# Attention and feed-forward layer on eight cores: order of score tiles in attention, queue of the reciprocal rows' write, PSUM banks of the down projection

## What is computed

```python
x = x + layernorm(attn(layernorm(x), w_qkv, w_out))
x = x + layernorm(ffn(layernorm(x), gate, up, down))
# attn: qkv = x @ w_qkv.T; per head and chunk of 512 queries, keys are the
# chunk before and its own (1024 keys; chunk 0 has 512); band mask
# j >= i and j <= i + 512; softmax(q k^T / sqrt(128)) @ v; then @ w_out.T
# ffn: W = (wq - 128) * scale; down(silu(gate(x)) * up(x))
```

## Time and profile before

| | us |
|---|---|
| runs shown | 4037.57 and 4462.24, median 4249.91 |
| the profiled execution | 4037.43 |
| its span, slowest core (core 1) | 4035.9 |
| spans of the eight cores | 4006.8 to 4035.9 |
| TensorE busy in the span | 3283.2 (81%) |
| VectorE, ScalarE, POOL busy | 1188.4, 813.9, 154.4 |

### The profile page before, as it was taken

How to read it: one execution, slowest core, us unless ns; L and a number is a source line. 1 busy time by engine, 2 the same in 40 slices (tenths; PEclk the granted TensorE clock), 3 DMA queues, 4 the chain that set the end, 5 groups by cost and what they waited for, 6 DMA issues and landing times.

```text
span 4035.9 us, 41674 instructions; the slowest of 8 cores (4006.8 to 4035.9 us)
## 1 busy us (share of the span) xinstructions
PE 3283.2 (81%) x16208; PEld 1526.1 (38%) x16208; DVE 1188.4 (29%) x1421; ACT 813.9 (20%) x1175; POOL 154.4 (4%) x208
## 2 busy tenths in 40 slices
PE   2578898898888843666599999999999869949886
PEld 1334444444444421233244444444444324414332
DVE  3434423423433443565511111111101111122223
ACT  1223323323323320212211111111111210020000
POOL 0000000000000000000000000000000000000000
PEclk9789999999999976887799999999999979979998
DMA  5221121121030034433211111111111233225655
GB/s 168 84 64 31 50 67 28 50 68 28 10 110 6 29 102 146 144 138 132 104 42 37 42 42 37 42 39 40 32 27 39 58 107 116 98 73 199 222 213 185
DMA packets 174800, 328.00 MB, mean 81 GB/s; under 512 B 9104, under 2 KB 131344, under 8 KB 154128
## 3 DMA queue, kind: packets, MB, share of 16 engines
q1 hardware_dynamic: 138128, 162.26, 13.1%
q0 software_dynamic: 23232, 115.36, 8.7%
q10 hardware_dynamic: 13248, 47.72, 3.5%
HBM read 243.38 MB, written 81.92 MB: 81 GB/s over the span
## 4 chain that ended last, share of the span: by engine, by line
PE 68%; DMA 13%; DVE 9%; issue 7%; ACT 2%; DVEq 0%; ACTq 0%; SPq 0%; POOL 0%; POOLq 0%
PE ps L871 15%; PE ps L889 15%; PE ps L388 11%; PE ps L950 9%; PE ps L347 6%; DMA ys<-SM 4%; PE ps L604 3%; DVE SM L593 3%; PE ps L518 2%; PE ps L528 2%; PE ps L697 2%; DMA CF<-ys 2%; PE ps L580 2%; DMA recs<-RCS 2%; DMA CF<-wdT 2%
## 5 line engine op out<-in xcount | busy, mean ns | idle before, releaser
L871 PE MATMUL ps<-AT,BB 128*128 128x512 bf16 x2816 | 617.8, 380 | 5.6 <-DVE BB L847 5.6
L889 PE MATMUL ps<-AT,BB 128*128 128x512 bf16 x2816 | 615.0, 379 | 0.0
L950 PE MATMUL ps<-BB,AT 128*128 128x512 bf16 x2048 | 466.8, 390 | 158.0 <-DVE SM L824 106.7
L388 PE MATMUL ps<-AT,BB 128*128 128x512 bf16 x2048 | 469.2, 383 | 2.5 <-ACT BB L398 2.5
L543 DVE TENSOR_REDUCE STT<-ps 128x1 f32<-128x1024 f32 (+1 forms) x256 | 268.0, 1087 | 630.0 <-PE ps L528 630.0
L871 PEld LDWEIGHTS ps<-AT,BB 128*128 128x128 bf16 x2816 | 276.4, 98 | 339.8 <-issue 9.6
L889 PEld LDWEIGHTS ps<-AT,BB 128*128 128x128 bf16 x2816 | 275.4, 98 | 332.4
L950 PEld LDWEIGHTS ps<-BB,AT 128*128 128x128 bf16 x2048 | 204.0, 100 | 417.8 <-issue 191.0
L697 PE MATMUL ps<-BB,SM 128*128 128x512 bf16 x1024 | 255.7, 416 | 114.0 <-ACT SM L716 99.6
L904 DVE TENSOR_TENSOR SM<-SM 128x2048 bf16<-128x2048 bf16 x44 | 53.9, 1225 | 980.6 <-ACT SM L899 980.6
L550 ACT ACTIVATE SM<-ps,STT 128x1024 bf16<-128x1024 f32 (+1 forms) x256 | 258.0, 1008 | 253.3 <-DVE STT L543 238.6
(11 more groups left out here) (92 smaller groups left out, 1872.3 us busy)
## 6 DMA issues: line engine op xcount, KB each, us to landing
AT<-zTs SPq DMA_DIRECT2D x32, 1408.0 KB, 9.0
CF<-wqkvT SPq DMA_DIRECT2D x36, 1024.0 KB, 10.5
CF<-x POOLq DMA_DIRECT2D x32, 1024.0 KB, 7.0
zTs<-SM POOLq DMA_DIRECT2D x44, 512.0 KB, 4.8
CF<-woutT SPq DMA_DIRECT2D x16, 1024.0 KB, 6.2
CF<-recs ACTq DMA_DIRECT2D x16, 1024.0 KB, 4.8
x1s<-SM POOLq DMA_DIRECT2D x16, 1024.0 KB, 5.0
ys<-SM POOLq DMA_DIRECT2D x32, 512.0 KB, 4.9
```

The lines of the kernel that those rows point to most:

```text
L388: ins = e.matmul(ps1[:, _nn * 512:(_nn + 1) * 512], _w[:, k * P:(k + 1) * P], h1T(k, _h2 * 1024 + _nn * 512, 512), start=(k == 0), stop=(k ...
L871: ins = e.matmul(ps0[:, n * 512:(n + 1) * 512], BB[:, (_base + k // 4) * 2048 + (k % 4) * 512 + _htl * P: (_base + k // 4) * 2048 + (k % 4 ...
L889: ins = e.matmul(ps1[:, n * 512:(n + 1) * 512], BB[:, (_base + k // 4) * 2048 + (k % 4) * 512 + _htl * P: (_base + k // 4) * 2048 + (k % 4 ...
L950: ins = e.matmul(_pso[:, n * 512:(n + 1) * 512], _zz[:, kt * P:(kt + 1) * P], wd_ap(kt)[:, n * 512:(n + 1) * 512], start=(kt == 0), stop=( ...
```

## The change

Three edits. In attention, the loop over tiles is cut into `emit_smm` (scores) and `emit_soft` (maximum and exponential). A chunk now emits: scores of tiles 0 and 1; the transposes and V product of the chunk before; a fill unit; softmax of tiles 0 and 1; a fill unit; scores of tiles 2 and 3; softmax of tiles 2 and 3. Banks, tiles and instructions stay as they are. In the projection, the write of the reciprocal row is issued by POOL instead of SP. In the down projection, row tiles alternate between banks 0, 1 and banks 2, 3 instead of going through all four pairs.

```diff
-                for t in range(4):
+                def emit_smm(t):
...
                     tr.emit("PE", smm,
                             reads=[qT_pg, kT_pg, rMK, rIDB], writes=sc_bks)
 
+                def emit_soft(t):
+                    reg = (t % 2) * 1024
+                    sc_bks = [bank[2 * (t % 2)], bank[2 * (t % 2) + 1]]
...
-                    if t == 1:
-                        drain_fill(1)
-
+
+                emit_smm(0)
+                emit_smm(1)
                 flush_tp()
                 drain_fill(1)
+
+                emit_soft(0)
+                emit_soft(1)
+                drain_fill(1)
+                emit_smm(2)
+                emit_smm(3)
+                emit_soft(2)
+                emit_soft(3)
...
-            dma("SY", rec_d[st2].rearrange("(a c) -> a c", a=16),
+            dma("GP", rec_d[st2].rearrange("(a c) -> a c", a=16),
                 RCS[0:16, :], "recw", reads=[rRCS],
...
-                q4 = st % 4
-                pb = [bank[2 * q4], bank[2 * q4 + 1]]
-                pso = (ps0 if q4 < 2 else ps1)[
-                    :, (q4 % 2) * 1024:(q4 % 2) * 1024 + 1024]
+                pb = bank[0:2] if st % 2 == 0 else bank[2:4]
+                pso = ps0[:, 0:1024] if st % 2 == 0 else ps0[:, 1024:2048]
```

## The result

The kernel became slower: the ratio of its time to that of the kernel before is 1.0384, with a 95% interval of 1.0366 to 1.0402. The median of the eleven executions is 4191.39 us; the profiled one took 4184.07 us around a span of 4182.5 us, 146.6 us more than the profiled execution before. The forecast, 4239 us, had reckoned +202 us on the same base, so it had the direction and, as will be seen, the waits one by one, but about a third too much time. Some executions of either kernel are longer by several per cent, with one die at a lower granted clock, and the ratio leaves them out. The median of two times that was given before the forecast, 4249.91 us, is not a base to set the forecast of 4239 beside: it would even look like a small gain. The forecast's own base, 4037.4, was the right one.

The account below looks back on a forecast made before the run. Attention was taken as bound by TensorE, the projection's period as set by its reciprocal-row write and load loop. 4037.4 + 187 (attention order) + 15 (write on POOL) + 0 (banks) = 4239 us, own range 4185 to 4300.

Parts of the forecast that it names:

- The sum for a head at full clock, 71.25: One attention head: 7.8 + 14.55 + 18.9 + 18.9 + 11.1 us, 6.3 more than the 64.9 measured before.
- The clock term: Attention: 3.1 falls to half clock per head at 1.75 us each, 5.4 us on top of 71.25.
- a little over 1.5, since transposes slow too: Attention: price of one fall to half clock, 1.75 us, taken from a 1.5 us loss in a V product.
- every junction falls: Attention: by the idle-gap rule alone, the clock drops to half at each junction; rows agreed for chunk 2, not chunk 3.
- Times 16: Attention: 11.7 us more per head, counted alike for all 16 heads, +187 us.
- I take 1 us more per write: Projection: each of 16 reciprocal-row writes lands 1 us later on POOL's queue, +15 us.
- B: Attention: the clock falls no more than today, +126 us, plus 15 for the write, 4178 us; chance 0.15.
- C: Attention: clock stays low through transposes, V and into the units at every junction, +325 us, 4377 us in all; chance 0.13.
- D: Attention: not slower; transposes and V run without waits for copies and the clock holds, 3981 us; chance 0.08.
- E: Projection: POOL's queue holds the write for the x load or VectorE, landing 7.0 us, 4266 us in all; chance 0.08.

Follow-up runs that it names:

- the run with filler in both waits: Changed kernel's attention order alone, plus useless matmuls in the waits for the exponential and for the last copy before V; 1.0224 to the kernel before.
- the run with the moved unit: New attention order with the second fill unit moved behind scores and softmax of tiles 2 and 3; 0.9848 to the kernel before.
- The run with maxima first: New attention order, but softmax of tiles 0 and 1 emitted ahead of the previous chunk's transposes; 1.0543 to the kernel before.

## Why the prediction was right and where it was wrong

The mechanism of the slowdown was right. Two terms of the sum were wrong: the half clock was put at 5.4 us per head and cost 3.5 to 3.9, and the write on POOL was put at 15 us and showed no cost.

**The order is slower (edit 1): right, by its own mechanism.** Banks 0 to 3 make the next chunk's scores wait for exponentials, and the head's end waits for its own softmax. The lengths were 1.44, 1.97 + 0.27, 2.04 + 0.27 and 3.34 us where the forecast had 1.6, 2.3 + 0.4, the same again, and 3.6. The sum for a head at full clock, 71.25, was met by the run with filler in both waits (71.0 to 71.7). Moving one unit into the gap took away the whole loss and more.

**The clock term: its mechanism and the number of falls right, its price too high.** The forecast took 3.1 falls per head at 1.75 us, 5.4. Three of five stretches fell, and were 1.1, 1.0 and 1.9 us longer than the forecast's figures at full clock. The first two were 0.2 shorter, so the head shown lost 3.9, and the ordinary head of 74.7 us lost 3.5. The step that failed is the price, "a little over 1.5, since transposes slow too". The 1.5 came from a V product, which is paid in full, and so is the fall at the head's end, which covers V. The other two lie in scores and transposes, behind which stand waits for copies; slower transposes use up these waits (0.27 us is left of the 0.49 and 0.19 that the run with the moved unit shows). That is 1.5 to 1.9 us per head, 24 to 30 us in all. The run with maxima first is consistent with this. The rule on idle gaps that the forecast cites from the Trainium skill (page TensorE: Matmul & The Clock Gate, section HAM oscillation) is told there of waits longer than those inside this kernel's junctions, so it does not give "every junction falls"; and the first junction, with waits of 1.44 and 1.40 us, kept 1.00.

**Times 16: too generous.** The ordinary head grew by 9.8 us (64.9 to 74.7), times 16 = 157; attention grew by 149.5. By the starts of the heads, the first grew by 7.3 us, the last, up to its last product with V, by 7.5, and heads 3 to 5 (the first is 0) by 25.0 in sum instead of 29.5, while others grew by up to 12.4. This is 8 us and was not followed further.

**The write on POOL (edit 2): wrong as a central value, +15 us.** The failed step is "I take 1 us more per write": on POOL the write landed no later. Over the eight cores the medians are 3.1 to 3.9 us in the changed kernel's trace and 3.5 to 4.3 in the one before, the projection is 436 us on the mean in both, and on the slowest cores the projection and what lies ahead of it changed by -1.1 us together. That a later landing would cost about its own length in every step is not refuted: where the write and the load of the attention output both landed 1.0 to 1.3 us later, the projection took 16 to 18 us more (table above). No run separates the two transfers. Removing the wait for the landing altogether gained 0.7 us per step.

**The banks (edit 3): right, 0**, for the reason given: 19 us to spare.

Together what was too large, some 38 us in attention (the price of the falls and the times 16) and some 18 in the rest (15 and the small changes of the other stages), is the 55 us between +202 and +147. Of the rivals, B (no more falls than today, 4178) came closer in its number and is refuted in its mechanism: the clock fell in three stretches and filling the waits regained 53 us. C is refuted by an attention clock of 0.92. D is refuted: transposes and V still wait 98 us for copies. E is refuted by the landing, 3.9 us and not 7.0. Only B names a time near the measured one, and that nearness is luck: too few falls and 15 us for a write that cost nothing made up for each other.

## What to carry to other kernels

Count, for each wait that an order of work creates, what independent work stands behind it in the queue and could stand before it: here one 3.5 us unit in the gap between two uses of the same PSUM banks turned +3.6% into -1.5%. Price a wait of TensorE with the clock that it costs, and look where the half-clock stretch falls: on work with a wait behind it, it is partly free, on a stream of long matmuls it is paid in full. Removing the wait for a transfer that the chain of waits names is worth only what the next late thing leaves of it, so look for that one before multiplying.

## What the runs showed that was not expected

Useless matmuls, 1.7 us of them in each wait for softmax and 0.87 us in each wait for the last copy, held the clock at 0.99 and gained 53 us. In the first of these waits alone they mostly did not hold it (heads of 74.9 us beside two of 70.9).

The issue of a write on POOL takes 0.5 us or 1.0 to 1.2, by what VectorE does. Seven of the 16 in the changed kernel are short: four beside nothing, three that start with less than 0.4 us of VectorE's tensor_scalar (L780) to go. The nine long ones start with 0.9 to 1.1 us of it to go. One of each:

```profile
1827.27 1.35 DVE L780 TENSOR_SCALAR SM<-SM,STT 128x2048 bf16<-128x2048 f32 x1 [0.18 <-DVE STT L281]
...
1828.33 0.50 POOL L247 DMA_DIRECT2D recs<-RCS  x1 [5.73 <-ACT RCS L674]
```

```profile
1853.80 1.35 DVE L780 TENSOR_SCALAR SM<-SM,STT 128x2048 bf16<-128x2048 f32 x1 [0.18 <-DVE STT L281]
1854.04 1.20 POOL L247 DMA_DIRECT2D recs<-RCS  x1 [4.92 <-ACT RCS L674]
```

In the first VectorE is near its end when the issue starts, in the second it has 1.1 us to go, and the issue ends with it. This agrees with the Trainium skill, page SBUF — State Buffer, section SBUF: two separate sides, on descriptors that wait while VectorE holds the shared port. The 0.6 us that it adds did not show in the time.
